# Six layers of windowed attention and feed-forward on one core: the rounds of the main part written out instead of looped

## The chip, the cores and the metric

The kernel runs on one core of a Trainium2 chip. The metric is device time in microseconds: the median of several executions. One execution was also taken with the hardware profiler; its span and every row below come from that one.

## The reference, cut to what matters

```python
x = x + attn_ref(layernorm(x), w, w_out)          # linear attention with a running sum over T
x = x + ffn_ref(layernorm(x), Wqkv, ..., W2, b2)   # six layers of the following
for i in range(6):
    x = attn_layer(shift_tokens(x), Wqkv[i], q_scale[i], k_scale[i], Wo[i]) + x
    x = ffn_layer(shift_tokens(x), ln_g[i], ln_b[i], W1[i], b1[i], W2[i], b2[i]) + x
# attn_layer: qkv = x @ Wqkv; l2norm of q and k per head (16 heads of 64); rotary;
#             softmax attention in windows of 32 tokens with the window before; @ Wo
# ffn_layer:  layernorm, @ W1, a * gelu(gate), @ W2
```

x is 16 batches of 256 tokens of 128 channels, float32. The change touches only the six-layer part.

## The kernel before, in words

The whole of x lies in SBUF with channels on partitions. The program has a first part (row norm, linear attention, row norm), then the main part, then a short tail that adds the result back. The change is in the main part.

A unit of work is one batch in one layer; there are 6 x 16 = 96. A unit passes four stages, each a round later than the one before: lag 0 (projection to q, k and v, rotary, norm, transposes of q and k), lag 1 (windowed attention), lag 2 (output projection, layernorm, the first matmul of the feed-forward), lag 3 (the rest of the feed-forward). One round is one call of `body`, and does lag 0 of a unit, lag 1 of the unit before, and so on. So a round keeps four units in flight, and 99 rounds do it all.

The five engines (TensorE, VectorE, ScalarE, GpSimd, and SyncE that issues the DMAs) each run their own program. What an engine does in a round, in which order, is written by hand in the table `ORDER`; `run_slots` walks it. Nothing is planned by a cost model. Each engine calls the same function, `pipeline`, with its own `body`, and the loops are there:

- rounds 1 to 3 are written out (the pipeline fills);
- then an outer loop over layers 0 to 4 (`eng.Fori(0, DEPTH - 1)`), whose body is: SyncE's `loads` of the next layer's weights; an inner loop over 13 rounds (`eng.Fori(3, NB)`); `conv_a`, in which ScalarE and VectorE turn the loaded weights of the next layer into the forms that the matmuls read; and three rounds written out, which also do the rest of that conversion (`wa` and `wc` in `ORDER`);
- then an inner loop of 13 rounds for layer 5, and three rounds written out that drain the pipeline.

Engines meet at semaphores that only count up. `Count.at(batch, n)` gives the value to wait for: batch times the counts per batch, plus n. In a loop `batch` is a register, so that the value is worked out by register instructions of the engine's sequencer. `hold` (line 378) is a wait followed by an increment of a semaphore that nobody waits for (`pe_held`, `sp_held`). TensorE uses it 13 times a round: ahead of each of the four bursts of 64 matmuls of `b_qk` (line 667) and ahead of the four bursts of 64 of `b_pv` (line 701), where there are one or two more. SyncE uses it in `loads`.

TensorE's lines by which a round is recognised: line 630 is the first matmul of a projection tile, the first thing of a round; 645 to 647 project v; 654 transposes q and k; 677 and 711 transpose probabilities and outputs; 719 is the output projection; 752 and 759 the feed-forward.

Of the kernel before, what the change touches and what calls it, by code (L numbers as in the profile page):

```python
# [29 lines left out]
NB, T, D = 16, 256, 128  # L30
NT = T // P
DEPTH, HEADS, DH, WIN = 6, 16, 64, 32
# [65 lines left out]
def build(nc, x_in, w_in, w_out_in, Wqkv, q_scale, k_scale, Wo, ln_g, ln_b, W1, b1, W2, b2,  # L98
          rotary, masks, ident_in, pick_in, gather_in, seg_in, out):
    ctx = ExitStack()  # L100
    with ctx:
# [195 lines left out]
        def pipeline(eng, body, conv_a=None, loads=None):  # L297

            body(1, 0, (0,), 0, None)
            body(2, 1, (0, 1), None, None)
            body(3, 2, (0, 1, 2), None, {2: 0})
            with eng.Fori(0, DEPTH - 1) as l:
                loads and loads(l + 1)
                with eng.Fori(3, NB) as g:
                    body(l * NB + g + 1, g, (0, 1, 2, 3), None, {2: l, 3: l})
                conv_a and conv_a(l + 1)
                body(l * NB + NB + 1, 0, (0, 1, 2, 3), l + 1, {2: l, 3: l})
                body(l * NB + NB + 2, 1, (0, 1, 2, 3), None, {2: l, 3: l}, (2, l + 1))  # L310
                body(l * NB + NB + 3, 2, (0, 1, 2, 3), None, {2: l + 1, 3: l}, (3, l + 1))
            last = (DEPTH - 1) * NB
            with eng.Fori(3, NB) as g:
                body(last + g + 1, g, (0, 1, 2, 3), None, {2: DEPTH - 1, 3: DEPTH - 1})
            body(last + NB + 1, 0, (1, 2, 3), None, {2: DEPTH - 1, 3: DEPTH - 1}, end=1)
            body(last + NB + 2, 1, (2, 3), None, {2: DEPTH - 1, 3: DEPTH - 1}, end=2)
            body(last + NB + 3, 2, (3,), None, {3: DEPTH - 1})
# [60 lines left out]
        def hold(eng, held, s, value):  # L378

            eng.wait_ge(s, value)
            eng.sem_inc(held, 1)

        def bank_free(eng, a, n):

# [12 lines left out]
        def _(sp):  # L398
# [116 lines left out]
            def loads(layer):  # L515

                hold(sp, sp_held, w_lo, 3 * layer)
                hold(sp, sp_held, w_c, 4 * layer)
                load_weights(layer)

            load_x(0)
            pipeline(sp, body, loads=loads)

            sp.wait_ge(x_stored.sem, x_stored.at(DEPTH * NB, 16))
# [5 lines left out]
        def _(pe):  # L530
# [126 lines left out]
            def b_qk(b, u):  # L657
                t, par = UNIT[u]
                if u == 0:

                    pe.wait_ge(trA_copied.sem, trA_copied.at(b, 8))
                hold(pe, pe_held, mask_put.sem, mask_put.at(b, u + 1))
                for m in range(8):
                    for w in range(4):
                        col = m * 2 * WIN
                        q0 = t * P + w * WIN
                        mm = pe.matmul(b_sim[w * WIN:(w + 1) * WIN, col:col + 2 * WIN],  # L667
                                       qT[64 * par:64 * par + 64, m, q0:q0 + WIN],
                                       kT[64 * par:64 * par + 64, m, q0:q0 + 2 * WIN],
                                       start=False, stop=w == 3 and m == 7, skip_group_check=True)  # L670
                mm.then_inc(sim_full.sem, 1)
# [105 lines left out]

            steps["fin"] = fin_tr_
            pipeline(pe, lambda *z, **k: run_slots(steps, "pe", *z, **k))
            fin_tr_(7)  # L780

        @block.scalar
        def _(act):
# [163 lines left out]
            for k in range(4):  # L948
                w_cs(0, 0, k)
            steps.update({"wa": w_a, "wc": w_cs})  # L950
            pipeline(act, lambda *z, **k: run_slots(steps, "act", *z, **k), conv_a)

# [401 lines left out]
```

## Time and profile before

| what | value |
|---|---|
| median of 3 runs | 3637.79 us (3636.72 to 3644.33) |
| the profiled execution's own time | 3636.09 us |
| its span, first to last instruction | 3634.3 us |
| TensorE busy | 3397.6 us (93%) |
| VectorE busy | 3109.7 us (86%) |
| ScalarE busy | 2520.1 us (69%) |
| GpSimd busy | 1849.6 us (51%) |
| mean granted TensorE clock | 0.979 |

Busy time leaves out register, branch, semaphore and DMA-issuing instructions. "Issue" as the cause of an idle time means that the engine waited for nothing that the profile shows. Times in rows count from the start of the span.

### The profile page before, as it was taken

To read this page: it belongs to the slowest core of one execution; us is meant where nothing else is said; L and a number is where in the kernel's file an instruction comes from. 1 tells how busy PE (TensorE), PEld (TensorE's weight loads), DVE (VectorE), ACT (ScalarE), POOL (GpSimd) and SP (SyncE) were. 2 spreads that over 40 slices of the span, in tenths; PEclk is the share of its full clock that TensorE was granted. 3 is DMA by queue.
4 is the path that set the end of the run, shared out by engine and by line. 5 is a ranking of instruction groups with operands and counts; after the bars stand their busy time and mean duration, and the time that the engine had idled before them with its cause. 6 is when DMAs were issued, how large, how long until landed. Compare 5 with 4: busy or idle time off the path is not lost.

```text
span 3634.3 us, 161649 instructions
## 1 busy us (share of the span) xinstructions
PE 3397.6 (93%) x63524; PEld 2729.1 (75%) x63524; DVE 3109.7 (86%) x6016; ACT 2520.1 (69%) x4543; POOL 1849.6 (51%) x1604
## 2 busy tenths in 40 slices
PE   5857999999999999999999999999999999999997
PEld 2325888878788877788887788887788887788885
DVE  8987888888788888788888788888788888888884
ACT  2015777777777777777777677777677777777774
POOL 1434655554555555456555465555455564555561
PEclk9988999999999999999999999999999999999998
DMA  2002423323333323333233432332423332323333
GB/s 83 12 26 54 103 60 79 75 57 82 87 77 77 71 62 77 89 79 74 57 79 70 96 75 60 76 78 56 107 63 73 79 73 61 77 66 70 79 75 79
DMA packets 186363, 261.00 MB, mean 72 GB/s; under 512 B 31670, under 2 KB 89908, under 8 KB 185396
## 3 DMA queue, kind: packets, MB, share of 16 engines
q1 hardware_dynamic: 186164, 258.24, 31.6%
q8 instruction: 138, 2.26, 0.3%
q14 instruction: 61, 0.50, 0.1%
HBM read 22.30 MB, written 4.19 MB: 7 GB/s over the span
## 4 chain that ended last, share of the span: by engine, by line
PE 83%; issue 8%; DVE 5%; ACT 1%; POOL 1%; SPq 1%; DMA 0%; DVEq 0%; ACTq 0%; POOLq 0%
PE bank L667 10%; PE bank L654 9%; PE bank L719 9%; PE obank L701 8%; PE bank L752 7%; PE bank L630 7%; PE bank L632 5%; PE bank L631 5%; PE bank L677 5%; PE bank L711 4%; PE bank L645 3%; PE bank L759 3%; PE bank L647 2%; PE bank L646 2%; PE bank L739 1%
## 5 line engine op out<-in xcount | busy, mean ns | idle before, releaser
L977 POOL TENSOR_TENSOR qn<-qn,rinv 128x512 f32<-128x512 f32 x768 | 799.0, 1056 | 1305.0 <-DVE rinv L1224 1305.0
L971 POOL TENSOR_TENSOR qn<-ropec,ropes 128x512 f32<-128x512 f32 x768 | 991.3, 1302 | 257.6 <-DVE ropes L1176 216.1
L852 ACT ACTIVATE sq<-bank 128x512 f32<-128x512 f32 x768 | 458.3, 598 | 195.9 <-PE bank L632 169.3
L1184 DVE TENSOR_REDUCE ss<-sq 128x8 f32<-128x512 f32 x768 | 496.4, 676 | 84.8 <-ACT sq L852 84.8
L1175 DVE TENSOR_TENSOR ropec<-bank,rots 128x512 f32<-128x512 f32 x768 | 525.0, 684 | 18.5 <-ACT sq L852 12.1
L1176 DVE TENSOR_TENSOR ropes<-bank,rots 128x512 f32<-128x512 f32 x768 | 521.6, 679 | 0.0
L654 PE MATMUL bank<-ident,qn 128*128 128x128 f32 x3072 | 470.9, 276 | 26.1 <-ACT qT L870 18.8
L654 PEld LDWEIGHTS bank<-ident,qn 128*128 128x128 f32 x3072 | 369.3, 142 | 94.9 <-POOL qn L977 26.1
L667 PEld LDWEIGHTS bank<-kT,qT 64*32 64x32 f32 x24576 | 362.9, 107 | 96.5 <-issue 96.1
L667 PE MATMUL bank<-kT,qT 64*32 64x64 f32 x24576 | 422.2, 217 | 12.6 <-issue 6.7
L630 PE MATMUL bank<-wqkv_hi,xs_hi 128*128 128x512 f32 x768 | 365.5, 476 | 66.8 <-issue 42.7
L876 ACT ACTIVATE bank<-mask_f 128x512 f32<-128x512 f32 x384 | 231.8, 604 | 199.3 <-DVE Pr L1235 188.8
L719 PE MATMUL bank<-OT,wo 128*128 128x256 f32 x1536 | 357.2, 385 | 0.7 <-DVE x L1278 0.7
L701 PE MATMUL obank<-V,PT 64*32 64x65 f32 x24576 | 333.5, 225 | 9.5 <-issue 9.5
L701 PEld LDWEIGHTS obank<-V,PT 64*32 64x32 f32 x24576 | 269.2, 105 | 75.4 <-issue 75.4
L719 PEld LDWEIGHTS bank<-OT,wo 128*128 128x128 f32 x1536 | 283.9, 190 | 44.4 <-issue 1.0
L752 PE MATMUL bank<-xn,w 128*128 128x256 f32 (+1 forms) x1152 | 309.1, 391 | 2.7 <-DVE hm L1272 2.7
L859 ACT ACTIVATE Vt<-bank 128x512 f32<-128x512 f32 x384 | 225.2, 586 | 121.6 <-PE bank L647 121.6
L632 PE MATMUL bank<-wqkv_hi,xs_lo 128*128 128x512 f32 x768 | 309.4, 403 | 0.0
L631 PE MATMUL bank<-wqkv_lo,xs_hi 128*128 128x512 f32 x768 | 307.9, 401 | 0.0
L1235 DVE TENSOR_TENSOR Pr<-bank,mx 128x512 f32<-128x512 f32 x384 | 265.3, 691 | 45.3 <-DVE mx L1230 2.4
L1230 DVE TENSOR_REDUCE mx<-bank 128x8 f32<-128x512 f32 x384 | 262.8, 684 | 47.1 <-PE bank L667 46.9
(138 smaller groups left out, 6239.6 us busy)
## 6 DMA issues: line engine op xcount, KB each, us to landing
V<-Vt SPq DMA_DIRECT2D x576, 260.0 KB, 4.4
V<-Vt SPq DMA_DIRECT2D x192, 130.0 KB, 4.5
V<-Vt SPq DMA_DIRECT2D x192, 65.0 KB, 4.1
xres<-X SPq DMA_DIRECT2D x96, 128.0 KB, 2.1
X<-x SPq DMA_DIRECT2D x96, 128.0 KB, 2.0
wqkv_raw<-L_ffn_Wqkv SPq DMA_DIRECT2D x6, 1536.0 KB
xraw<-X SPq DMA_DIRECT2D x97, 64.0 KB, 2.0
xraw<-X SPq DMA_DIRECT2D x97, 63.8 KB, 1.9
```

The lines of the kernel that those rows point to most:

```text
L630: pe.matmul(o, xs_hi[:, rows], wqkv_hi[:, cols], start=True, stop=False)
L632: pe.matmul(o, xs_lo[:, rows], wqkv_hi[:, cols], start=False, stop=True).then_inc(proj_full.sem, 1)
L654: mm = pe.transpose(b_trA[:, j * P:(j + 1) * P], qn[:, c, j * P:(j + 1) * P], ident[:])
L667: mm = pe.matmul(b_sim[w * WIN:(w + 1) * WIN, col:col + 2 * WIN], qT[64 * par:64 * par + 64, m, q0:q0 + WIN], kT[64 * par:64 * par + 64, m ...
L701: mm = pe.matmul(obank[w * WIN:(w + 1) * WIN, slot, j * 65:j * 65 + 65], PT[rows, u % 2, j * P + w * WIN:j * P + (w + 1) * WIN], V[rows, w ...
L719: mm = pe.matmul(b_c[:, 0:T], wo[:, i, :], OT[:, i, :], start=i == 0, stop=i == 7)
L752: mm = pe.matmul(b_c[0:n, part * T:(part + 1) * T], w1[:, cols], xn[:], start=True, stop=True)
L971: pool.tensor_tensor(qn[:, c, :], ropec[:, c % ROPE_RING, :], ropes[:, c % ROPE_RING, :], ALU.add).then_inc(rope_sum.sem, 1)
L977: pool.tensor_tensor(heads8(qn[:, c, :]), heads8(qn[:, c, :]), rinv[:, 8 * c:8 * c + 8].unsqueeze(2).broadcast_to([P, 8, DH]), ALU.mult).t ...
L1175: dve.tensor_tensor(halves(ropec[:, c % ROPE_RING, :]), raw, table(t, 2 * kind), ALU.mult)
L1176: dve.tensor_tensor(halves(ropes[:, c % ROPE_RING, :]), raw[:, :, ::-1, :], table(t, 2 * kind + 1), ALU.mult).then_inc(roped.sem, 1)
L1184: dve.tensor_reduce(ss[:, 8 * c:8 * c + 8], heads8(sq[:, c % 2, :]), AX.X, ALU.add).then_inc(ss_done.sem, 1)
```

## The change

Each `eng.Fori` of `pipeline` becomes a loop of Python, so that all 99 rounds are in the program of every engine, one after another, with no branch between them. The layer `l` and the batch `g` are then plain numbers, every semaphore value that a round waits for is a constant, and the addresses of the DMAs too. In `hold` the increment is left out where the value is a plain number. The loop of the first part (`la_pipeline`) stays a loop.

```diff
-            with eng.Fori(0, DEPTH - 1) as l:
+            for l in range(DEPTH - 1):
                 loads and loads(l + 1)
-                with eng.Fori(3, NB) as g:
+                for g in range(3, NB):
                     body(l * NB + g + 1, g, (0, 1, 2, 3), None, {2: l, 3: l})
                 conv_a and conv_a(l + 1)
                 body(l * NB + NB + 1, 0, (0, 1, 2, 3), l + 1, {2: l, 3: l})
                 body(l * NB + NB + 2, 1, (0, 1, 2, 3), None, {2: l, 3: l}, (2, l + 1))
                 body(l * NB + NB + 3, 2, (0, 1, 2, 3), None, {2: l + 1, 3: l}, (3, l + 1))
             last = (DEPTH - 1) * NB
-            with eng.Fori(3, NB) as g:
+            for g in range(3, NB):
                 body(last + g + 1, g, (0, 1, 2, 3), None, {2: DEPTH - 1, 3: DEPTH - 1})
...
             eng.wait_ge(s, value)
-            eng.sem_inc(held, 1)
+            if not isinstance(value, int):
+                eng.sem_inc(held, 1)
```

## Rows read from the trace of the kernel before

**Rows 1.** The page: busy time of each engine, and the chain that ended last.
```profile
PE 3397.6 (93%) x63524; PEld 2729.1 (75%) x63524; DVE 3109.7 (86%) x6016; ACT 2520.1 (69%) x4543; POOL 1849.6 (51%) x1604
PE 83%; issue 8%; DVE 5%; ACT 1%; POOL 1%; SPq 1%; DMA 0%; DVEq 0%; ACTq 0%; POOLq 0%
```

**Rows 2.** TensorE's timeline: first instruction of a round (start, duration, idle before).
```profile
371.55 0.49 PE L630 MATMUL bank<-wqkv_hi,xs_hi 128*128 128x512 f32 x1 [0.25 <-issue]
406.64 0.49 PE L630 MATMUL bank<-wqkv_hi,xs_hi 128*128 128x512 f32 x1 [0.35 <-issue]
...
773.65 0.49 PE L630 MATMUL bank<-wqkv_hi,xs_hi 128*128 128x512 f32 x1 [0.32 <-issue]
812.74 0.79 PE L630 MATMUL bank<-wqkv_hi,xs_hi 128*128 128x512 f32 x1 [3.79 <-DVE xs_lo L1165]
849.04 0.50 PE L630 MATMUL bank<-wqkv_hi,xs_hi 128*128 128x512 f32 x1
882.35 0.50 PE L630 MATMUL bank<-wqkv_hi,xs_hi 128*128 128x512 f32 x1
921.58 0.79 PE L630 MATMUL bank<-wqkv_hi,xs_hi 128*128 128x512 f32 x1 [3.91 <-issue]
958.51 0.49 PE L630 MATMUL bank<-wqkv_hi,xs_hi 128*128 128x512 f32 x1 [0.34 <-issue]
...
2539.09 0.50 PE L630 MATMUL bank<-wqkv_hi,xs_hi 128*128 128x512 f32 x1
2578.37 0.79 PE L630 MATMUL bank<-wqkv_hi,xs_hi 128*128 128x512 f32 x1 [4.05 <-issue]
2616.59 0.49 PE L630 MATMUL bank<-wqkv_hi,xs_hi 128*128 128x512 f32 x1 [0.35 <-issue]
...
3091.99 0.50 PE L630 MATMUL bank<-wqkv_hi,xs_hi 128*128 128x512 f32 x1
3126.01 0.49 PE L630 MATMUL bank<-wqkv_hi,xs_hi 128*128 128x512 f32 x1 [0.23 <-issue]
3161.09 0.50 PE L630 MATMUL bank<-wqkv_hi,xs_hi 128*128 128x512 f32 x1 [0.28 <-issue]
...
3494.22 0.49 PE L630 MATMUL bank<-wqkv_hi,xs_hi 128*128 128x512 f32 x1 [0.26 <-issue]
```

**Rows 3.** DMA queues: the whole span, then rounds from 440.0, 849.0 and 882.4.
```profile
q8 instruction: 138, 2.26, 0.3%
...
q1 hardware_dynamic: 1568, 2.39, 32.6%
...
q8 instruction: 5, 0.08, 1.2%
...
q14 instruction: 6, 0.05, 0.5%
```

**Rows 4.** TensorE's timeline where it stands still inside or ahead of a burst.
```profile
843.78 0.50 PE L647 MATMUL bank<-wqkv_hi,xs_lo 128*128 128x512 f32 x1 [1.15 <-issue]
...
949.85 0.33 PE L701 MATMUL obank<-V,PT 64*32 64x65 f32 x10 [0.72 <-issue]
...
954.99 0.45 PE L701 MATMUL obank<-V,PT 64*32 64x65 f32 x29 [1.18 <-issue]
...
1467.96 0.63 PE L654 MATMUL bank<-ident,qn 128*128 128x128 f32 x4 [1.75 <-ACT qT L870]
...
3154.78 0.30 PE L667 MATMUL bank<-kT,qT 64*32 64x64 f32 x3 [1.66 <-issue]
```

**Rows 5.** Windows: stretch, its length, busy us and count of each engine, clock, DMA.
```profile
874.60:876.30 1.70, 1.70 (x130) 1.60 (x129) 1.50 (x7) 1.63 (x4) 0.00 (x0) 1.00 0.00 0
840.22:843.77 3.55, 2.41 (x131) 1.88 (x130) 3.00 (x12) 1.57 (x4) 1.00 (x1) 1.00 0.02 5
904.61:908.50 3.89, 3.89 (x124) 3.38 (x127) 3.35 (x8) 3.34 (x8) 0.00 (x0) 1.00 0.15 45
949.84:954.98 5.14, 3.97 (x124) 3.47 (x125) 3.40 (x9) 1.81 (x5) 4.07 (x4) 1.00 0.29 92
918.10:924.90 6.80, 3.32 (x9) 2.64 (x10) 1.72 (x3) 2.17 (x5) 3.40 (x4) 0.50 0.02 5
```

## The prediction

> **What bounds the kernel now.** I read the page first: TensorE is busy 93% of the span, VectorE 86%, and the chain that ended last is 83% TensorE and 8% "issue", time in which the engine waited for nothing that the profile shows [rows 1]. A change that only touches how instructions reach the engines can live on the issue part and on nothing else. So the next view was TensorE's timeline, for the start of each round. It shows four kinds of round [rows 2].
>
> A round in the inner loops lasts (773.65 - 406.64) / 11 = 33.36 us, and in layer 5 (3494.22 - 3161.09) / 10 = 33.31 us. TensorE is idle in it for 0.32 us, at its start, and there the loop branches back: this is the inner loop's price, and it is small. A round that is already written out, with all four stages and no branch behind it, lasts 882.35 - 849.04 = 33.31 us. The third written-out round of a layer, behind which the outer loop branches back, lasts 921.58 - 882.35 = 39.23 us, and at its end TensorE stands 3.91 us with the cause "issue". The same code in layer 5, where no outer branch follows, lasts 3126.01 - 3091.99 = 34.02 us. That pair is the heart of the forecast. Last, the first round of an inner loop: 406.64 - 371.55 = 35.09 us in layer 0, 3161.09 - 3126.01 = 35.08 us in layer 5, but 958.51 - 921.58 = 36.93 and 2616.59 - 2578.37 = 38.22 us behind the first and the last of the four outer branches.
>
> **What straight code costs.** Fetching is not free. Between the idle gaps that end at 949.85 and at 954.99 [rows 4] lie 124 matmuls and 125 weight loads [rows 5], some 256 instructions with the waits; the two gaps are of the same kind, in the middle of a burst of line 701. So a piece is about 256 instructions, the next is asked for when the one before it is entered, and TensorE stalls if it runs through a piece faster than the next arrives. The rows bracket that arrival: a piece of 3.55 us had a stall of 1.15 us in it [rows 4, 5], one of 3.89 us had none [rows 5]; so it needs some 3.3 to 3.8 us. While the weights of the next layer load, it needs 5.14 us [rows 5]. A round is 656 matmuls, 656 weight loads and about 25 semaphore waits, so 5.2 pieces and 6.4 us for an average one: hidden. But the fast part is not even: 259 instructions went through in 1.70 us where a burst of line 701 is followed by one of line 667 [rows 5].
>
> **The change part by part**, against the profiled execution's 3636.1 us.
>
> (a) The outer branch goes, 4 times. The round ahead of it should become like its twin in layer 5: 39.23 - 34.02 = 5.2 us (the four are 39.18 to 39.41), so 4 x 5.25 = 21.0 us. Two idle times make it up: 3.91 us of TensorE's own branch [rows 2], and about 1.7 us of waiting for ScalarE's copy of a transpose [rows 4], because ScalarE has branched too.
>
> (b) The round behind it. After the idle time TensorE ran at half the granted clock for 6.8 us: 0.50, that is 1.2 GHz instead of 2.4 [rows 5]. Layer 0's first looped round, which loads weights as well but has no branch ahead of it, takes 35.09 us, the four others 37.65 on average (36.93 to 38.22): 4 x 2.55 = 10.2 us.
>
> (c) The inner branch goes, in 72 rounds (78 less the first of each layer). The limits of a round without it are 33.31 us, the written-out one, and 33.04 us, the looped one less its 0.32 us of idle. What holds the written-out one at 33.31 is other engines: the time saved at the branch is waited for elsewhere. It still has register waits and extra weight copies on ScalarE, so I take 33.2: 60 x 0.16 + 12 x 0.11 = 10.9 us; both ends are 4 and 22 us.
>
> (d) Constants instead of registers. The register instructions sit on sequencers that run ahead of their engines. The 13 increments of `hold` a round go too, and with them TensorE can queue a burst's weight loads before its wait is met. I cost all of this at nothing beyond (c): the twin comparison contains it, and what hides it is TensorE's 33 us of matmuls in a 33.3 us round [rows 2]. If that cover were gone it would be a tenth of a microsecond at each of 13 places a round, a gain. SyncE's DMAs keep their number, order and waits: nothing.
>
> (e) Fetch stalls in the 72 rounds that had none. By the starts of all matmuls of the round from 849.04 to 882.35, about 84 of the positions where a piece may begin make it last under 3.5 us, mostly those that hold the 1.70 us pair, and they are short by 0.7 us on average. With a begin at each 256th instruction that is 84 / 256 x 0.7 = 0.23 us a round at 3.5 us of arrival, 0.17 at 3.3, 0.34 at 3.8, before what a stall gives back to the next piece. I take 0.2: 14.4 us lost. The ends are 0.05 (4 us) and 0.5 (36 us), since 1337 instructions a round and pieces of 256 nearly repeat every nine rounds, and which positions come up depends on a few instructions that I can't see yet. Here a stall is paid in full: layer 5's first looped round is 35.08 - 33.31 = 1.77 us longer, with a stall of 1.66 us in it [rows 2, 4].
>
> (f) The first looped rounds: in layer 5 that stall becomes an average one, 1.5 us gained. In the others a weight load makes stalls likely at any position: no change. The wait at 812.74 for converted weights (3.79 us [rows 2]) hangs on ScalarE's and VectorE's work after the last projection and stays.
>
> The sum: 3636.1 - 21.0 - 10.2 - 10.9 - 1.5 + 14.4 = 3606.9 us. The profiled execution was 1.7 us under the median of the runs, so I predict 3608.6, say 3608 us.
>
> The Trainium skill (Runtime: NRT & Kernel Launch, section Instruction fetch mechanics) says that fetching ahead is sequential, that a taken branch to code outside the two resident pages forces a fetch before execution goes on, and so that written-out code is preferable. For the outer branch the trace agrees (3.91 us). For the inner one it does not: by two pages of 16 KiB each of the 78 returns would fetch, and no instruction packet stands in a looped round. The same section calls the crossing of a page boundary mostly hidden; by that, (e) would be nothing, which is the first rival below, and the 1.15 and 1.66 us stalls speak against it.
>
> **The rivals.**
> 1. Fetching is wholly hidden in plain rounds: (e) is nought, and 3608 becomes 3594. For it: two written-out rounds in a row (849.04, 882.35) have no fetch stall. Against: the gaps of rows 4. Chance 0.15.
> 2. Slower: the pieces come too late as a rule. The fast stretches of a round run at 3.9 us a piece (3.89 in rows 5), so a small lengthening of the arrival makes several pieces a round stall and not one in three. Were it 4.5 us, halfway to the 5.14 us under weight loads, the same count gives 1.16 us a round, 84 us in all, and 3608 - 14 + 84 = 3678 us. It outweighs the 43.6 us of gains from 0.6 us a round on, which is an arrival of about 4.1 us. Against: the piece of 3.89 us without a stall, and that the DMA engines are nearly idle (0.02) in the fast part of a plain round [rows 5]. Chance 0.09.
> 3. The outer loop's end is slow for the weight loads and conversions and not for the branch, and stays: (a) and (b) are nought, 3608 + 31 = 3639 us. For it: layer 5's twin converts nothing for a next layer after it. Against: the loads are issued after the branch, and "issue" names no engine. Chance 0.06.
> 4. What is saved at branches is waited for elsewhere and stalls take the rest: within a few us of 3637. Chance 0.05.
>
> **How the numbers follow.** My case has 0.65, with its own range of 3590 to 3628 from the ends of (c) and (e). Rival 1 lies at 3594. The range that should hold 8 in 10 takes in rival 1 and the upper end of (e): 3590 to 3634. Below it is a steady round near 33.04 with hidden fetches, above it rivals 2 and 3. About 0.2% (7 us) can be told from no change. Faster by more: my case nearly whole and rival 1, 0.79. Within it: rivals 3 (mostly) and 4 and the edge of my case, 0.11. Slower: rival 2 and a little of rival 3, 0.10.
>
> **What the profile after would show.** q8 with about 500 pieces (99 rounds x 5.2) instead of 138, and no round without them. No idle time of 3.7 to 4.2 us with "issue" ahead of line 630, and no half clock behind it; the third round of layers 0 to 4 near 34 us. Plain rounds in two kinds: most near 33.2 us, some 0.5 to 1.3 us longer with an "issue" gap inside a 701 or 667 burst, about one in three. If every plain round has such gaps, (e) was mis-sized and rival 2 holds. If third rounds still take 39 us, (a) was wrong. If plain rounds stay at 33.3, (c) was.

## The result, and the profile after

The changed kernel takes 3589.91 us, the median of four runs (3582.8 to 3590.66), against 3637.26 us for the kernel before (four runs, 3634.12 to 3644.33). The ratio is 0.9862, with an interval of [0.9849, 0.9874]: 47 us gained where 29 were forecast. The sign was right; 3589.91 us lies just under the range, whose lower end was 3590, and so outside it. The profiled execution, whose rows follow, is the lowest of the four: 3582.8 us, span 3579.8.

The page of the kernel after, to be held against [rows 1] and the first line of [rows 3]:
```profile
PE 3386.0 (95%) x63524; PEld 2724.3 (76%) x63524; DVE 3116.5 (87%) x6016; ACT 2507.2 (70%) x4543; POOL 1846.9 (52%) x1604
q8 instruction: 505, 8.27, 1.0%
q14 instruction: 156, 1.28, 0.1%
PE 86%; issue 7%; DVE 4%; ACT 1%; POOL 1%; SPq 1%; DMA 0%; DVEq 0%; POOLq 0%; ACTq 0%
```
The counts of matmuls, weight loads and vector work are those of before to the last one. Only the fetching has changed: 505 pieces of TensorE's program where there were 138. TensorE's busy time fell by 11.6 us although it does the same matmuls: 7.4 us of it in the four rounds behind an outer branch, whose first matmuls no longer run at half the clock.

TensorE's timeline after, the first instruction of rounds (and, ahead of the second one, the last burst of the round before), to be held against [rows 2]:
```profile
405.24 0.50 PE L631 MATMUL bank<-wqkv_hi,xs_hi 128*128 128x512 f32 x1
...
437.40 0.86 PE L702 MATMUL obank<-V,PT 64*32 64x65 f32 x64
438.19 0.50 PE L631 MATMUL bank<-wqkv_hi,xs_hi 128*128 128x512 f32 x1
...
809.71 0.77 PE L631 MATMUL bank<-wqkv_hi,xs_hi 128*128 128x512 f32 x1 [2.91 <-DVE wqkv_lo L1066]
845.13 0.50 PE L631 MATMUL bank<-wqkv_hi,xs_hi 128*128 128x512 f32 x1
878.21 0.50 PE L631 MATMUL bank<-wqkv_hi,xs_hi 128*128 128x512 f32 x1
911.85 0.50 PE L631 MATMUL bank<-wqkv_hi,xs_hi 128*128 128x512 f32 x1
945.94 0.50 PE L631 MATMUL bank<-wqkv_hi,xs_hi 128*128 128x512 f32 x1
...
1348.32 0.77 PE L631 MATMUL bank<-wqkv_hi,xs_hi 128*128 128x512 f32 x1 [3.57 <-issue]
```
A plain round takes 438.19 - 405.24 = 32.95 us, not the 33.2 forecast. The third round of a layer takes 911.85 - 878.21 = 33.64 us where it took 39.23, the one behind it 945.94 - 911.85 = 34.09 where it took 36.93, and neither has idle time at its start. The 3.57 us at 1348.32 are not a branch: this is the wait for converted weights that stood at 812.74 before [rows 2]. It comes five times in both kernels: 18.2 us before, and after 17.4 us, 2.91 of them under DVE's name and 14.5 us under "issue" (the fifth "issue" of the row below, 4.04 us, is the start of the first round, as before). DVE is at work on the conversion of line 1066 when the wait ends. A releaser's name can change while the wait stays. The looped round that ended in this wait took 39.1 us before (773.65 to 812.74 [rows 2]) and takes 39.1 us after in four layers of five (40.35 us in layer 0, behind a fetch stall): there the branch that went has given nothing.

Windows of the kernel after (stretch, length, busy us and count of PE, PEld, DVE, ACT, POOL, clock, DMA share and GB/s): the place where the outer branch was, to be held against the last of [rows 5], and a plain round.
```profile
911.80:918.60 6.80, 6.80 (x108) 5.21 (x97) 5.70 (x12) 6.24 (x13) 6.80 (x8) 1.00 0.02 5
438.20:471.20 33.00, 33.00 (x662) 27.27 (x657) 29.39 (x59) 25.43 (x47) 18.23 (x17) 1.00 0.35 75
```
The clock stays at 1.00 (2.4 GHz) where it was 0.50, and in a plain round TensorE is busy for 33.00 of 33.00 us: the round is its matmuls and nothing else.

TensorE's waits in the kernel after (us in total, times, longest):
```profile
PE bank L631 <- issue: 18.6, 5, 4.0
PE bank L668 <- issue: 13.5, 15, 1.3
PE obank L702 <- issue: 7.5, 8, 2.9
```
The stalls of lines 668 and 702 are the fetch stalls of step (e). Counting all of TensorE's instructions from the start of the program, each such stall falls on a count of 196 or 197 modulo 256: pieces of exactly 256 instructions. A plain round has 1339 of them, 5.23 pieces.

The two profiled executions, summed over kinds of round (in us; the spans differ by 54.5):

| rounds | before | after | difference |
|---|---|---|---|
| 66 plain ones | 2201.3 (33.35 each) | 2187.1 (33.14 each) | -14.2 |
| 4 behind an outer branch | 150.6 (37.65) | 138.1 (34.52) | -12.5 |
| 4 that end in one | 157.1 (39.27) | 134.9 (33.71) | -22.2 |
| layer 5's first looped one | 35.07 | 33.76 | -1.3 |
| all others, start and tail | | | -4.3 |

A plain round is one of the looped ones other than the first and the last of a layer. The plain rounds hold two opposite terms: without a stall they fell from 33.35 to 32.95 us, which is -26.6 us over 66, and stalls and other excess gave back +12.4 us, 0.19 a round.

### The profile page after: what moved, and what is told of

Its sections match the earlier page's. It is cut to its first block, busy times and chain, and to the rows that moved or that the text cites. A ratio compares the mean times of both kernels' runs of the same rounds, so it can differ in the third digit from the quotient of the medians.

```text
span 3579.8 us, 150019 instructions
## 1 busy us (share of the span) xinstructions
PE 3386.0 (95%) x63524; PEld 2724.3 (76%) x63524; DVE 3116.5 (87%) x6016; ACT 2507.2 (70%) x4543; POOL 1846.9 (52%) x1604
## 4 chain that ended last, share of the span: by engine, by line
PE 86%; issue 7%; DVE 4%; ACT 1%; POOL 1%; SPq 1%; DMA 0%; DVEq 0%; POOLq 0%; ACTq 0%
PE bank L668 10%; PE bank L655 10%; PE bank L720 9%; PE obank L702 8%; PE bank L753 7%; PE bank L631 7%; PE bank L633 5%; PE bank L632 5%; PE bank L678 5%; PE bank L712 4%; PE bank L646 3%; PE bank L760 3%; PE bank L648 2%; PE bank L647 2%; PE bank L740 2%
## 5 line engine op out<-in xcount | busy, mean ns | idle before, releaser
L668 PE MATMUL bank<-kT,qT 64*32 64x64 f32 x24576 | 430.9, 217 | 18.4 <-issue 13.5
L871 ACT ACTIVATE kT<-bank 128x512 f32<-128x512 f32 x384 | 229.4, 597 | 73.4 <-PE bank L655 67.6
```

## The experiments

All times are medians; those of one chip are compared with the kernel before on that chip.

**after_again.** The changed kernel as it is, for its spread and to see whether the stalls come back in the same places.

> The changed kernel as it is, to be compared on one chip with the kernels beside it, and to see whether its executions lie at 3583 us, as the profiled one, or at 3590 us, as the three others. Both theories: 3583 to 3591 us; fetch stalls of some 0.7 to 1.3 us in about one plain round of five, all at the same place of the 256-instruction grid of TensorE's program.

Measured: 3588.83 us (3583.82 to 3592.58), ratio 0.9865 [0.985, 0.9881]. The stalls of the plain rounds stand at the same counts, with 9.4 us of excess in all where the first profile had 12.4. What differs most between executions are the six rounds in which weights load (206.6 us in one profile, 213.7 in the other): of the four behind the former outer branches two take 38.82 and 37.12 us here, with stalls of up to 2.3 us, where the first profile has none over 35.8.

**pad_good, pad_bad, pad_best, pad_worst.** Increments of a semaphore of TensorE that nobody waits for, behind the matmuls of line 720. Five a round make 1344 instructions, 5.25 pieces, so that the same four places of a round meet a piece's start over and over; the number for unit 3 (7, 34, 23, 50) chooses them (`c` counts units, and unit 3 passes these matmuls in round 5).
```
+                for _ in range(7 if c == 3 else 0 if c < 3 else 3 if c % 16 == 0 else 5):
+                    pe.sem_inc(pe_held, 1)
```

> TensorE gets 5 more semaphore increments a round behind the output projection (3 in the first round of a layer), 7 once at the start, so that a round is 1344 = 5.25 x 256 instructions and the 16 KB boundary falls on four places only, none of them where a burst of line 702 and one of 668 are run through within one piece. Theory that pieces of program arrive too late there: the stalls in plain rounds go, about 12 to 16 us less than the changed kernel, near 3575 us. Rival, that the idle times inside bursts have another cause (semaphores, weight loads): same time as the changed kernel, or slower by the 5 increments.

> The same 5 increments a round, but 34 once at the start instead of 7, so that one of the four places is the bad one and every fourth round meets it. Fetch theory: 23 rounds with a stall of about 1 us, so 20 to 28 us slower than the well-placed version and 8 to 12 us slower than the changed kernel, the idle times exactly every fourth round. Rival: within 3 us of the well-placed version.

Measured: 3584.68 us (3582.09 to 3589.03), ratio 0.9856 [0.9843, 0.987], and 3584.48 us (3580.87 to 3585.97), ratio 0.9851 [0.9838, 0.9865]. The difference expected between the two did not come. The reason is not that placement does nothing: the starts fell at instruction 989 of the round in the one and at 1026 in the other, and both stall: 8 of the plain rounds are longer by 0.5 to 1.4 us in the one, and every fourth by 0.3 to 0.9 us in the other. My limits of the sensitive stretch were off by some 16 instructions at either end. Together with the places in the kernel after (978 to 1021) they say where it lies: from about 976 to 1030, where a burst of line 702 is followed by one of line 668. That is narrower than the 64 instructions between two starts, so a choice with no stall exists (973 and 1037) and one in the middle (1010). Hence the next pair.

> As the version with 7 increments once at the start, but with 23, so that the four places of the 16 KB boundary move 16 instructions up. The traces so far show stalls of plain rounds only at places 978 to 1032 of a round (the last in question at 989, in every eighth round); the four places now are 973, 1037, 1101 and 1165 and their neighbours 256 away. Fetch theory: no stall over 0.3 us in a plain round, 8 to 10 us less than the version with 7, some 3575 us. Rival, that stalls come at some rate wherever the boundary falls: within 3 us of that version.

> The same with 50 increments at the start: one of the four places is 1010, in the middle of the bad stretch. Fetch theory: every fourth plain round stalls for 1.0 to 1.3 us, 20 to 28 us slower than with 23. Rival: same time.

Measured: pad_best 3573.43 us (3570.03 to 3574.65), ratio 0.9817 [0.9804, 0.9831]; pad_worst 3599.28 us (3595.91 to 3604.78), ratio 0.9892 [0.9877, 0.9907]. The two do the same work, with the same number of instructions in every round but the one of unit 3, and lie 26 us apart. First the waits, then the starts of three rounds on TensorE's timeline, of pad_best:
```profile
PE bank L668 <- issue: 4.8, 4, 3.0
PE obank L702 <- issue: 3.5, 5, 1.2
```
```profile
979.29 0.50 PE L631 MATMUL bank<-wqkv_hi,xs_hi 128*128 128x512 f32 x1
1012.24 0.50 PE L631 MATMUL bank<-wqkv_hi,xs_hi 128*128 128x512 f32 x1
1045.18 0.50 PE L631 MATMUL bank<-wqkv_hi,xs_hi 128*128 128x512 f32 x1
```
And of pad_worst:
```profile
PE bank L668 <- issue: 27.0, 26, 4.0
PE obank L702 <- issue: 8.8, 10, 2.1
```
```profile
987.51 0.50 PE L631 MATMUL bank<-wqkv_hi,xs_hi 128*128 128x512 f32 x1
...
1015.46 0.26 PE L668 MATMUL bank<-kT,qT 64*32 64x64 f32 x4 [1.10 <-issue]
...
1021.44 0.50 PE L631 MATMUL bank<-wqkv_hi,xs_hi 128*128 128x512 f32 x1
1054.43 0.50 PE L631 MATMUL bank<-wqkv_hi,xs_hi 128*128 128x512 f32 x1
```
And the 50 increments (line 723) in round 5 of pad_worst, with the matmuls ahead of them and the burst behind:
```profile
420.37 3.72 PE L720 MATMUL bank<-OT,wo 128*128 128x256 f32 x16
428.09 1.93 PE L668 MATMUL bank<-kT,qT 64*32 64x64 f32 x64 [3.99 <-issue]
...
L723 PEldq EVENT_SEMAPHORE  x50: 51/51/51, 420.4 to 428.0; - x50
```
In pad_best two rounds in a row take 32.95 and 32.94 us. In pad_worst a stall of 0.7 to 1.3 us comes every fourth round (1015.46, 1148.57), and its round takes 1021.44 - 987.51 = 33.93 us, the one behind it 32.99. Over the 66 plain rounds the excess above 32.94 is 2.2 us in the one and 26.0 in the other, and the spans of the two profiled executions differ by 27.6.

Not all of this is the place of the pieces. The fifth round of pad_worst alone takes 40.05 us, 7.1 too long, and its idle time of 3.99 us at 428.09 stands outside the pattern of 256. Its cause is the padding itself: TensorE's sequencer gets through one increment in 0.155 us, so 50 in a row take from 420.4 to 428.0, longer than the 3.72 us of matmuls queued ahead of them, and behind the idle time TensorE runs at a mean clock of 0.51 for 6.8 us. The 34 in a row of pad_bad end in an idle time of 1.53 us at the same place; the 23 of pad_best do not. Without that round the plain rounds differ by 16.7 us, and the second written-out rounds of the layers, which stall at the same count, by another 4.1 (170.1 against 166.0 us for five). The place of the pieces is thus worth some 20 of the 27.6 us, and the 20 to 28 us that were forecast were met with the help of a cost that the forecast did not have. Step (e)'s mechanism is shown all the same, and pad_best beats both kernels of this case: by 67 us the one before, and, going by the two ratios, by some 16 us the one after.

**hold_back.** The increment of `hold` is made at every wait again, in straight code.
```
-            if not isinstance(value, int):
-                eng.sem_inc(held, 1)
+            eng.sem_inc(held, 1)
```

> The changed kernel with the increment of hold put back (13 a round on TensorE). Theory that the plain round fell from 33.36 to 32.95 us because the branch went: the plain round stays at 32.95 to 33.05 us, the whole within 8 us of the changed kernel, the difference coming from other places of the 16 KB boundary. Rival, that the missing increments let TensorE run ahead: the plain round goes back to 33.2 to 33.3 us, 17 to 25 us slower.

Measured: 3594.62 us (3590.2 to 3599.47), ratio 0.9881 [0.9866, 0.9896], 6 us above the changed kernel (after_again, on the same chip), with intervals that overlap. TensorE's timeline of hold_back, two starts:
```profile
981.55 0.50 PE L630 MATMUL bank<-wqkv_hi,xs_hi 128*128 128x512 f32 x1
1014.52 0.50 PE L630 MATMUL bank<-wqkv_hi,xs_hi 128*128 128x512 f32 x1
```
A round without a stall takes 32.97 us here, and 32.94 at the least, so the increments, 13 of them spread over the round, cost nothing in it. They move the starts of the pieces (1347 instructions a round). Two of the four rounds in which weights load after layer 0 take 39.67 and 39.29 us; but the changed kernel has such rounds too, of 38.82 us in one execution and none over 35.8 in the other, so the 6 us are not shown to come from the moved starts. That the removed holds brought the gain is refuted.

**inner_out.** The kernel before, with the inner loops alone written out; the outer loop, the register waits and the increments stay.
```
-                with eng.Fori(3, NB) as g:
+                for g in range(3, NB):
```

> The kernel before with only the inner loops written out; the outer loop stays, so waits of layers 0 to 4 are still for register values and the increments of hold stay. Theory that the inner branch alone costs the 0.4 us a plain round: plain rounds at 32.95 to 33.05 us, some of them with a fetch stall, third rounds of layers 0 to 3 still near 39.3 us with half clock behind them; in all 15 to 20 us less than before, near 3620 us. Rival, that constants were needed: plain rounds of layers 0 to 4 at 33.2 to 33.3 us, no gain or a loss of up to 10 us.

Measured: 3647.9 us (3645.4 to 3653.39), ratio 1.0025 [1.0014, 1.0036]. It is slower than before, where a gain of some 20 us was expected. TensorE's timeline of inner_out:
```profile
874.09 0.24 PE L667 MATMUL bank<-kT,qT 64*32 64x64 f32 x2 [1.63 <-issue]
...
880.19 0.50 PE L630 MATMUL bank<-wqkv_hi,xs_hi 128*128 128x512 f32 x1
...
918.93 0.79 PE L630 MATMUL bank<-wqkv_hi,xs_hi 128*128 128x512 f32 x1 [3.50 <-issue]
...
949.22 0.32 PE L701 MATMUL obank<-V,PT 64*32 64x65 f32 x9 [2.00 <-issue]
...
959.70 0.63 PE L654 MATMUL bank<-ident,qn 128*128 128x128 f32 x4 [3.21 <-ACT qT L870]
...
961.05 0.51 PE L630 MATMUL bank<-wqkv_hi,xs_hi 128*128 128x512 f32 x1
...
995.95 0.50 PE L630 MATMUL bank<-wqkv_hi,xs_hi 128*128 128x512 f32 x1
1028.92 0.50 PE L630 MATMUL bank<-wqkv_hi,xs_hi 128*128 128x512 f32 x1
```
The plain round was right: 1028.92 - 995.95 = 32.97 us with register waits and increments in it, so constants are not needed for it. The plain rounds give 8.6 us in all. What the expectation missed is that the outer loop now runs over 16 rounds of straight code at the same addresses. The second written-out round of every layer has its piece start at the same place and stalls each time (874.09, 1430.11; 7.4 us in all), and the round behind the outer branch (918.93 to 961.05, 42.12 us; the four average 41.05) has the branch, a stall of 2.0 us or more in the weight loads, and a wait for ScalarE: 13.6 us lost. In the whole change both are gone (its second written-out rounds take 166.9 us for five, against 166.4 before and 173.8 here), which is why the whole change is worth more than its inner half.

**outer_out.** The kernel before, with the outer loop alone written out.
```
-            with eng.Fori(0, DEPTH - 1) as l:
+            for l in range(DEPTH - 1):
```

> The kernel before with only the outer loop written out, the inner loops of 13 rounds stay. Theory: the third rounds fall to 33.7 to 34 us and the half clock behind them goes, plain rounds stay at 33.36 us without fetch stalls: 32 to 36 us less than before, near 3604 us. Rival, that the third rounds are slow for the weight work: no change.

Measured: 3606.75 us (3604.07 to 3609.71), ratio 0.9906 [0.9891, 0.9922], 34 us less than before, as expected. Its timeline:
```profile
884.47 0.50 PE L630 MATMUL bank<-wqkv_hi,xs_hi 128*128 128x512 f32 x1
...
918.36 0.49 PE L630 MATMUL bank<-wqkv_hi,xs_hi 128*128 128x512 f32 x1
953.62 0.49 PE L630 MATMUL bank<-wqkv_hi,xs_hi 128*128 128x512 f32 x1 [0.28 <-issue]
...
2038.86 0.63 PE L667 MATMUL bank<-kT,qT 64*32 64x64 f32 x11 [3.60 <-issue]
```
The third rounds fell from 39.27 to 33.79 us (here 918.36 - 884.47 = 33.89): 21.9 us, step (a) by itself. The rounds behind them gave only 2.7 us in all (35.26, 35.77, 40.48 and 36.42 us); the 40.48 one holds the stall of 3.60 us at 2038.86, in the weight loads. Step (b)'s gain is therefore not fixed by the branch alone: it is what the fetch stalls of that round leave of it. The plain rounds, still looped, take 33.31 us, 0.04 less than before.

**small_copy.** The kernel before, where ScalarE's copy of the weights `wo` takes one column from layer 1 on instead of all (so the later layers project with stale weights). It tests what held the 33.31 us of the round from 849.04 [rows 2], on which step (c) rests.
```
-                    act.activation(wo[:], wo_raw[:], ACT.Copy).then_inc(w_c, 1)
+                    if isinstance(layer, int) and layer == 0:
+                        act.activation(wo[:], wo_raw[:], ACT.Copy).then_inc(w_c, 1)
+                    else:
+                        act.activation(wo[:, 0, 0:1], wo_raw[:, 0, 0:1], ACT.Copy).then_inc(w_c, 1)
```

> The kernel before, but ScalarE's copy of the output projection's weights (8 x 128 columns, line 932) is cut to one column from layer 1 on; so the output of later layers uses layer 0's matrix there. It stands in the written-out round that I took as the pattern of a round without a branch (33.31 us). Theory that this round was long for the copy: the idle time of 0.20 us ahead of the burst of line 667 at place 617 goes and the round is 33.0 to 33.1 us; the whole only 0 to 2 us less. Rival, that it is long for what any straight round pays: it stays at 33.3 us.

Measured: 3638.48 us (3632.97 to 3640.45), ratio 0.9995 [0.9985, 1.0005]. In the whole nothing, as it should be for five rounds. The round itself is what counts. TensorE's timeline of the kernel before, inside that round:
```profile
871.13 0.37 PE L667 MATMUL bank<-kT,qT 64*32 64x64 f32 x12 [0.23 <-ACT bank L876]
```
and of small_copy, its start and its end:
```profile
853.64 0.49 PE L630 MATMUL bank<-wqkv_hi,xs_hi 128*128 128x512 f32 x1
...
886.58 0.50 PE L630 MATMUL bank<-wqkv_hi,xs_hi 128*128 128x512 f32 x1
```
Before, TensorE waits 0.23 us there for ScalarE's mask, which is behind the copy. Without the copy the wait is gone and the round takes 886.58 - 853.64 = 32.94 us; the five are 32.93 to 33.01, against 33.29 on average. A straight round cost 32.97 us in the kernel before already. The pattern I had measured it by was not a plain one.

**pe_out and others_out.** The kernel before with the rounds written out for TensorE alone, and for the four other engines alone. A second copy of `pipeline` with Python loops is used by the engines named:
```
-            pipeline(pe, lambda *z, **k: run_slots(steps, "pe", *z, **k))
+            pipeline_flat(pe, lambda *z, **k: run_slots(steps, "pe", *z, **k))
```

> Only TensorE's rounds are written out; the four other engines keep both loops. Theory that the inner branch hurts on TensorE alone and the outer one on TensorE (3.9 us) and ScalarE (1.7 us): plain rounds at 32.95 us with the changed kernel's stalls, third rounds of layers 0 to 3 between 35 and 37 us, the whole some 3596 to 3606 us. Rival, that the others' branches cost nothing: 3590 us, as the changed kernel.

> The complement: TensorE keeps its loops, the four others are written out. Theory: plain rounds at 33.3 to 33.36 us with 0.3 us of idle time at the branch, third rounds near 37.5 us, the whole some 3625 to 3633 us. Rival, that the branches of the others cost nothing: 3637 to 3641 us, as before.

Measured: pe_out 3597.05 us (3593.88 to 3601.77), ratio 0.989 [0.9872, 0.9908]; others_out 3621.49 us (3619.21 to 3625.98), ratio 0.9955 [0.9937, 0.9972], 3.5 us below the range that was expected (3625 to 3633). The timeline of pe_out:
```profile
880.16 0.51 PE L653 MATMUL bank<-wqkv_hi,xs_hi 128*128 128x512 f32 x1
...
915.33 0.50 PE L653 MATMUL bank<-wqkv_hi,xs_hi 128*128 128x512 f32 x1
...
984.34 0.50 PE L653 MATMUL bank<-wqkv_hi,xs_hi 128*128 128x512 f32 x1
...
1017.30 0.51 PE L653 MATMUL bank<-wqkv_hi,xs_hi 128*128 128x512 f32 x1
```
and of others_out:
```profile
880.95 0.50 PE L653 MATMUL bank<-wqkv_hi,xs_hi 128*128 128x512 f32 x1
...
918.42 0.79 PE L653 MATMUL bank<-wqkv_hi,xs_hi 128*128 128x512 f32 x1 [3.75 <-issue]
955.46 0.49 PE L653 MATMUL bank<-wqkv_hi,xs_hi 128*128 128x512 f32 x1 [0.35 <-issue]
988.83 0.49 PE L653 MATMUL bank<-wqkv_hi,xs_hi 128*128 128x512 f32 x1 [0.32 <-issue]
```
TensorE's own program carries the plain round: 1017.30 - 984.34 = 32.96 us with the others looping, 988.83 - 955.46 = 33.37 us with TensorE looping. The third round splits as step (a) had it: 35.17 us on average when only the others branch (1.38 to 1.55 us of waiting for ScalarE's transposes is left), 37.61 when only TensorE does (3.65 to 4.05 us idle). Of its 39.27 us, 5.6 go when both are straight.

## Why the prediction was right in sign and short in size

**(a)** held: 21.0 us forecast, 22.2 in the profiles, 21.9 with the outer loop alone. Both parts were seen separately in pe_out and others_out. Rival 3, that the layer's end is slow for its weights and not for the branch, is refuted: the weight wait is still there (17.4 us in five), and the rounds behind the branch kept their 2.4 GHz.

**(b)** was 12.5 us for 10.2 forecast, with the half clock gone as said. The size was luck: the same program gave 4.7 us in after_again's profile, the same edit 2.7 us in outer_out, and in hold_back two of the four rounds took over 39 us. The half clock goes each time, the fetch stalls under the weight loads come and go.

**(c)** is the step that failed. It was put as a plain round going to 33.2 us, because "what holds the written-out one at 33.31 is other engines: the time saved at the branch is waited for elsewhere". It went to 32.95, below even the 33.04 end that I had given. Over the 66 plain rounds the floor's fall is worth 26.6 us, where the whole step had 10.9: 16 us, most of the distance from 3608 to 3590. The step also counted 72 rounds; the last looped rounds of layers 0 to 4 gained nothing (195.5 us for five before, 196.6 after), since they end in the wait for converted weights.

The written-out round was held by another engine indeed, but by a wait that only it has, for ScalarE behind its weight copy; small_copy takes it away and leaves 32.97. The prediction names those copies, but took off only 0.11 us for all that sets this round apart, when one look at the idle times inside it would have shown the ScalarE row. The other end, 33.04, was too high as well, since it took the idle time of 0.32 us for the whole price of the branch. TensorE's timeline of the kernel before, the last burst of a round and the start of the next:
```profile
438.81 0.86 PE L701 MATMUL obank<-V,PT 64*32 64x65 f32 x64
439.99 0.49 PE L630 MATMUL bank<-wqkv_hi,xs_hi 128*128 128x512 f32 x1 [0.32 <-issue]
```
From the burst's start to the round's it is 439.99 - 438.81 = 1.18 us here, and 438.19 - 437.40 = 0.79 us in the kernel after. The 0.39 us between them are nearly the whole 0.40 us a round. The profile counts idle time from the modelled end of the burst (439.67), while without the branch the next matmul starts 0.07 us ahead of that end.

**(d)** held: neither constants (inner_out has register waits and 32.95 us rounds) nor the missing holds (hold_back) move a plain round by more than 0.02 us. An increment does have a price, 0.155 us of the sequencer's time in pad_worst, and it shows where many stand in a row.

**(e)** held, in kind and in size: 0.2 us a round forecast, 0.19 measured (12.4 us for the 66; 0.14 in after_again), pieces of 256 instructions, stalls where a 702 burst meets a 668 burst. The count was not quite as drawn: the sensitive stretch is some 54 places wide, not 84, with stalls nearer 0.9 us than 0.7, and about one round in four and a half (15 of 66) is longer by over 0.2 us, not one in three. Rival 1 (nothing stalls) nearly has the time that came out, 3594, but for the wrong reason: the stalls are there. pad_best shows what it would have been worth. The ends given for (c) and (e), 22 us gained and 4 us lost, together reach down to 3587; the range of my case, 3590 to 3628, was drawn tighter than its own terms. Rival 2 (every piece late) is refuted, and rival 4 as well.

**(f)** held: 1.3 us for 1.5.

Against the prediction's 29.2 us the two profiles differ by 54.5: (c) has 15.7 us of the 25.3 between them, (b) 2.3, (e) 2.0, (a) 1.2, less 0.2 for (f). Smaller terms that I had not counted give 4.3 us; and the profiled execution lies 7 us under the median of its runs, so the terms of one profile sum to more than the medians show.

## What to carry to other kernels

Before a round of one kind is used as the price of another, list the idle times inside it and say for each whether the other kind has it; 0.25 us a round (33.2 against 32.95), times 66, is 16 of the 18 us by which the forecast missed the median. An idle time is only the least that a branch costs: measure from start to start. When a loop of tens of microseconds is written out, TensorE gains its branch and begins to fetch, and where the pieces of 256 instructions start decides part of the gain: make the round's count a multiple of 64 with a few idle increments and move the start out of the densest bursts, and measure two offsets. Keep the increments few at one place: 23 in a row were free here, 34 left TensorE idle for 1.53 us and 50 for 3.99. Writing out the inner loop and keeping the outer one can lose, since each pass meets the same unlucky starts and the branch is still paid.

## What the runs showed of the hardware that I had not expected

- The same matmuls differ by 26 us (3573.43 and 3599.28 us) with 27 more increments on a semaphore, once. In the profiles some 20 of 27.6 us come from where the 256-instruction pieces start, and 7 from the increments' own time (0.155 us each) and the half clock behind them.
- While a layer's weights load, a stall can be much longer than in a plain round: 3.69 us in hold_back, 3.60 us in outer_out, 2.0 to 2.9 us in inner_out, against 0.4 to 1.8 us in plain rounds. A stall that long brings the clock down as the branch did: the 6.8 us behind the one of 3.60 us have a mean clock of 0.53, those behind the one of 2.00 us (949.22 in inner_out) 0.75, and those behind the one of 1.10 us (1015.46 in pad_worst) keep 1.00. The window of outer_out:
```profile
2038.90:2045.70 6.80, 6.80 (x93) 5.72 (x93) 2.50 (x5) 3.01 (x6) 6.80 (x7) 0.53 0.01 3
```
- Looped, TensorE's round of some 1380 instructions brings no instruction packet at all [rows 3], more than five pieces of 256, and the return costs 0.40 us a round in all (33.35 against 32.95). The outer loop's body, some 5490 instructions, is fetched again at each return. The Trainium skill (Runtime: NRT & Kernel Launch, section Instruction fetch mechanics) speaks of a window of two pages, outside which a taken branch forces a fetch; by that the inner return would fetch, and the trace disagrees. The prediction stopped there, but the same section gives TensorE an instruction memory of 128 KiB, 2048 instructions, and with that size the trace agrees: the loop that stays is shorter, the one that is fetched again is longer. The same section calls the crossing of a page boundary mostly hidden. By the count that is so here, since about one boundary in twenty stalls, but those few cost the kernel after some 12 us, and some 20 us lie between the best and the worst place for them.
